# Handing out per-node factors by a matmul: fp32 operands replaced by three exact bf16 parts

## The reference, cut to what matters

```
h        = einsum('ni,hio->hno', layernorm(x), W)
z        = leaky_relu(attn_src[:, src] + attn_dst[:, dst])
weight   = exp(z - max(z))
out[dst] = sum over edges of weight / (sum of weight at dst + 1e-10) * h[src]
```

## Time and profile before

| what | value |
|---|---|
| median of 3 runs | 6532.46 us (6529.53 to 6537.09) |
| the profiled execution | 6535.86 us |
| its span, first to last instruction | 6534.1 us |
| mean granted TensorE clock | 0.889 |

### The profile page before, as it was taken

One profiled execution on the slowest core, in us unless ns is written; L12 is line 12 of the kernel. 1 busy time (PEld: TensorE's weight loads), 2 busy tenths in 40 slices (PEclk: granted clock), 3 DMA queues, 4 the chain that ended last, 5 costly groups with the idle time before them and its releaser, 6 DMA issues. The chain is left out here.

```text
span 6534.1 us, 98546 instructions
## 1 busy us (share of the span) xinstructions
PE 5150.2 (79%) x32067; PEld 4637.9 (71%) x32068; DVE 4163.5 (64%) x9813; ACT 1761.5 (27%) x4052; POOL 4122.6 (63%) x4039
## 2 busy tenths in 40 slices
PE   4438999999999999999995666666666666665887
PEld 3328999999999999999994554554455555455887
DVE  6437899899899889989983333343343343334666
ACT  2202444444444444444441000000000000003554
POOL 1357766776777767677654777777777777771111
PEclk9658999999999999999997777777777777787999
DMA  6555555555555565556543444444444444443121
GB/s 190 151 151 150 152 159 151 154 157 150 155 156 155 149 154 159 150 153 159 150 121 92 128 134 127 128 134 126 125 130 123 121 124 119 118 120 107 64 77 49
DMA packets 639144, 877.37 MB, mean 134 GB/s; under 512 B 254782, under 2 KB 447376, under 8 KB 638050
## 3 DMA queue, kind: packets, MB, share of 16 engines
q0 software_dynamic: 183392, 501.66, 27.2%
q1 hardware_dynamic: 424972, 334.16, 19.6%
q10 hardware_dynamic: 30326, 35.87, 1.6%
HBM read 766.70 MB, written 155.49 MB: 141 GB/s over the span
## 5 line engine op out<-in xcount | busy, mean ns | idle before, releaser
L1231 POOL DMA_INDIRECT m_ring<-tab_a,m_src x1764 | 1970.2, 1117 | 849.5 <-issue 489.4
L1849 POOL DMA_INDIRECT eb_rows<-tab_b,eb_src x1764 | 1714.9, 972 | 541.2 <-issue 537.0
L2090 PE MATMUL eb_acc<-eb_rows,eb_S 128*128 128x257 f32 x3528 | 1131.9, 492 | 505.6 <-DMA eb_rows<-tab_b,eb_src 504.4
L2090 PEld LDWEIGHTS eb_acc<-eb_rows,eb_S 128*128 128x128 f32 x3528 | 884.5, 256 | 714.6 <-DMA eb_rows<-tab_b,eb_src 530.8
L1512 PE MATMUL m_acc<-m_V,m_S 128*128 128x264 f32 x3528 | 862.5, 390 | 0.0
L1916 DVE TENSOR_TENSOR eb_sum<-eb_acc,eb_sum 128x257 f32<-128x257 f32 x98 | 41.8, 426 | 1232.2 <-PE eb_acc L2090 1232.2
L1512 PEld LDWEIGHTS m_acc<-m_V,m_S 128*128 128x128 f32 x3528 | 648.4, 192 | 93.0
L1633 ACT ACTIVATE mh_high<-m_ps,bn_b,bn_s 128x256 fp32r<-128x256 f32 x784 | 441.5, 563 | 891.7 <-PE m_ps L533 891.7
L521 DVE TENSOR_TENSOR mh_low<-mh_full,mh_high 128x512 fp32r<-128x512 f32 x784 | 543.3, 693 | 63.8 <-ACT mh_full L1633 49.6
L1622 ACT ACTIVATE mh_full<-m_ps,bn_b,bn_s 128x256 f32<-128x256 f32 x784 | 400.6, 563 | 664.5 <-DVE mh_low L521 342.0
L1307 DVE TENSOR_TENSOR m_V<-m_ring,m_V 128x1280 f32<-128x1280 f32 (+1 forms) x392 | 532.8, 1359 | 13.4
(11 more groups left out here) (367 smaller groups left out, 10539.9 us busy)
## 6 DMA issues: line engine op xcount, KB each, us to landing
m_dstb<-dst_p SPq DMA_DIRECT2D x196, 320.0 KB
m_dstb<-dst_p SPq DMA_DIRECT2D x196, 256.0 KB
buf<-empty SPq DMA_DIRECT2D x49, 771.0 KB
m_ring<-tab_a,m_src POOLq DMA_INDIRECT x1764
eb_rows<-tab_b,eb_src POOLq DMA_INDIRECT x1764, 2.8
xw_stage<-in_L_ffn_w_dram ACTq DMA_DIRECT2D x16, 1024.0 KB, 9.0
over<-b_blank SPq DMA_DIRECT2D x9, 1452.0 KB, 15.3
mOV<-over SPq DMA_DIRECT2D x49, 264.0 KB, 4.8
```

The lines of the kernel that those rows point to most:

```text
L1231: gp.indirect_dma_start(out=ring[:, j, :], out_offset=None, in_=scratch["tab_a"], in_offset=bass.IndirectOffsetOnAxis(ap=src[:, j:j + 1], ...
L1849: gp.indirect_dma_start(out=rows_[q.par][j][:, t, 0:D], out_offset=None, in_=scratch["tab_b"], in_offset=bass.IndirectOffsetOnAxis(ap=src_ ...
L2090: last_i = nc.tensor.matmul(ps_acc[j][:, 0:NR], S[q.par][j][:, t, :], rows_[q.par][j][:, t, :], start=t == 0, stop=t == WT - 1)
```

## The change

The 16 factors are no longer kept as fp32 for the fused stage: in `bounds`, after the second list is made and before the remaining weight pieces are split, five DVE instructions cut `q` into three bf16 numbers whose sum is the fp32 number (`split_q`). The fp32 `q` lives only through the early phases. The mask `ST` becomes bf16 and keeps the order of the list, so that it is read and written without a step, and a piece of it is now a stationary operand whose columns lie five or four bf16 numbers apart. The hand-out of a piece becomes three bf16 matmuls, which are added in PSUM, each with its own weight load of the same mask. Four pairs of small tiles are also put in one tile each, without another effect on the instructions.

```
-            k["q"] = sbuf(first, "q", [P, NT + 1, 2 * H])
+            k["q3"] = sbuf(first, "q3", [P, NT, 3, 2 * H], BF16)
...
+                k["q"] = sbuf(early, "q", [P, NT + 1, 2 * H])
...
+            def split_q():
+
+                v.wait_ge(q_ok, 2)
+                q, part = k["q"][:, 0:NT, :], [k["q3"][:, :, i, :] for i in range(3)]
+                step(nc.vector.tensor_copy(part[0], q))
+                step(nc.vector.tensor_tensor(q_left[:, :, :], q, part[0], SUB))
+                step(nc.vector.tensor_copy(part[1], q_left[:, :, :]))
+                step(nc.vector.tensor_tensor(q_left[:, :, :], q_left[:, :, :], part[1], SUB))
+                step(nc.vector.tensor_copy(part[2], q_left[:, :, :]))
...
             make_list(1, blist)
+            split_q()
             for n in range(4, len(stages)):
                 lower(n)
...
-    ST = [sbuf(ctx, f"m_ST{i}", [P, QUARTERS[i], P]) for i in pair]
+    ST = [sbuf(ctx, f"m_ST{i}", [P, P, QUARTERS[i]], BF16) for i in pair]
...
-                nc.vector.tensor_scalar(
-                    ST[s.side][:, 0:s.size, :], dstb[s.side][:, 0:s.size * P].rearrange("q (p c) -> q c p", c=s.size),
-                    node_col[s.par][:, :], None, ALU.is_equal).then_inc(ST_ok, 1)
+                nc.vector.tensor_scalar(ST[s.side][:, :, :].rearrange("q p c -> q (p c)"), dstb[s.side][:, 0:s.size * P],
+                                        node_col[s.par][:, :], None, ALU.is_equal).then_inc(ST_ok, 1)
...
-                    last_i = nc.tensor.matmul(psE[s.side][:, j * 16:j * 16 + 2 * H], ST[s.side][:, j, :],
-                                              k["q"][:, s.n, :], start=True, stop=True)
+                    for i in (2, 1, 0):
+                        last_i = nc.tensor.matmul(psE[s.side][:, j * 16:j * 16 + 2 * H], ST[s.side][:, :, j],
+                                                  k["q3"][:, s.n, i, :], start=i == 2, stop=i == 0)
```

More of the change, by code:

```diff
@@ L591, in bounds @@
     zm = sbuf(ctx, "b_zm", [P, 2])
+    q_left = sbuf(ctx, "b_q_left", [P, NT, 2 * H])
     corr = k["corr"]
@@ L1120, in attend_mix @@
     lg = [sbuf(ctx, f"mlg{i}", [P, GM, NX]) for i in pair]
-    lm = [sbuf(ctx, f"mlm{i}", [P, GM]) for i in pair]
-    ls = [sbuf(ctx, f"mls{i}", [P, GM]) for i in pair]
     wg = [sbuf(ctx, f"mwg{i}", [P, GM, NX]) for i in pair]
@@ L1126, in attend_mix @@
     mv = [sbuf(ctx, f"mmv{i}", [P, GM, 2]) for i in pair]
-    ve = [sbuf(ctx, f"mve{i}", [P, GM]) for i in pair]
-    rs = [sbuf(ctx, f"mrs{i}", [P, GM]) for i in pair]
+    ve, rs, lm, ls = ([x[:, i, :] for i in pair] for x in (sbuf(ctx, "m" + n, [P, 2, GM]) for n in ("ve", "rs", "lm", "ls")))
     h1 = [Split(sbuf, ctx, f"mh1{i}", [P, KB, T2]) for i in pair]
```

## The result

The median of four runs is 6387.68 us (6378.63 to 6391.94), the ratio to the kernel before 0.9775 with an interval of 0.9760 to 0.9791. The change makes the kernel faster by 2.25%, 145 us; 201 were forecast. The profiled execution took 6378.63 us, its span 6376.8, the granted clock was 0.886. Of its 157 us against the profiled execution of before, 152.7 lie between the first and the last output bias, so in the fused stage.

What follows compares the result with a forecast made beforehand. PE was taken to set the fused stage's period. The profiled 6535.86 us, less 208 for the hand-out matmuls, plus 7 for the split, gave 6335, so 6331 for the median; the 8-in-10 range was 6290 to 6450.

Steps and rivals of the forecast that it cites:

- What bounds the kernel: Fused stage: PE sets the group's period of 60.55 us, DVE stands 10% below, POOL 14%.
- The pair: Hand-out on PE: a strided bf16 load and matmul takes 27 ns, the contiguous price, against 0.103 us for fp32 before.
- The rule weighed against it: Skill on PE weight loads: packed or strided columns load fast, supporting 27 ns; its general figure is 107 ns for 128.
- The exit's 0.09 us: First two fp32r pairs behind a hand-out take 0.32 instead of 0.23 us; this delay was left as it is.
- The mask: On DVE, beside PE: 1.412 and 0.682 us fall to 553 and 486 ns, 4.2 us a group, priced at nothing.
- part 1: Hand-out matmuls on PE's path: 0.556 us less a quarter on average, 375 times, 208 us in all.
- The split: Five DVE instructions in `bounds`, on the path: 7 us more, nothing hides them; between 3 and 10.
- The first: Rival: strided mask loads on PE stay at 0.103 us a pair, slower than before, 6715 us; chance 0.13.
- The second: Rival: the step doubles PE's load cost, pairs of 50 ns, 6447 us; chance 0.12.
- The third: Rival: DVE takes over, mask at one number a cycle, or POOL loses its slack to the masks: 6387 us; chance 0.12.
- What would show it: Output bias every 56 us, pairs 25 to 29 ns, POOL's staging wait about a third; wrong if pairs exceed 40 ns.

Runs made afterwards that it cites:

- experiments 9 and 10: A small GpSimd addition behind each quarter's gathers, on the changed kernel with one matmul a piece (6449.77 us) and with 128 consecutive edges a piece (6457.94 us).
- experiment 2: Changed kernel with the bf16 mask written piece by piece again, so each piece's load is contiguous and the mask slow: 6417.49 us.
- experiment 3: Changed kernel with mask columns 6, 2, 8 and 16 bf16 numbers apart and the first part of q used three times: 6447.76 us.

## Why the prediction was right or wrong

- **What bounds the kernel: right.** PE set the period before and sets it after; what its hand-outs lost, the group lost: from the start of each of their matmuls to the next start they took 7.38 us a group before and 4.11 after, 3.27 less, and the period is 3.31 shorter. Two readings were a little off, and nothing hangs on them: PE reaches nine tenths from the fifth slice, not the fourth, and the stretch to 3500 us reaches past the stage; up to 3200 us POOL's pauses before the change are 9.9 us a group, not 9.4, and DVE's waits 4.1, not 4.6. That POOL's wait for staging was slack holds too: the additions of experiments 9 and 10 used it up whole.
- **The pair: the mechanism right, the price wrong; this is the term that was mis-sized.** I took the 27 ns of contiguous columns for columns 8 and 10 bytes apart, with the argument that a 16-byte step costs VectorE nothing. VectorE's reading says nothing about TensorE's weight load: measured are 35 and 41 ns. Nor was the reading right: it set the mask (682 ns with a 16-byte step) against another kind of instruction (685), and without the step the mask takes 495. The bounds were right (27 to 103), the choice at their lower end was not. In the sum it is 208 - 152.7 = 55 us of the 57 by which the median lies above the forecast.
- **The rule weighed against it.** By their step, strided bf16 loads take 26 to 63 ns a pair. The Trainium skill ("TensorE: Matmul & The Clock Gate", "Weight-path perf modes") says that columns may be packed or strided; here strided columns are loaded faster than fp32 ones, but not at the packed price from four numbers on. Its general figure for a load (section "LDWEIGHTS"), 107 ns for 128 columns, is not reached at any step. The page agreed with my choice but names no price for a step, and there was no row that did.
- **The exit's 0.09 us: right.** It is still there (0.32 for the two fp32r pairs).
- **The mask: right within 5%.** 580 and 495 ns against 553 and 486. It was right too that it buys nothing by itself and is the cover for part 1: without it (experiment 2) the group takes 58.12.
- **The split: the right size, the wrong exposure.** 6.7 us as worked out, at the place named; but "nothing hides them" was wrong, only 2 to 3 of them reach the end of the phase. I had "3 if ACT's loads catch up" as an end of the range and did not take it.
- **The rivals.** The first is out: no bf16 step reaches 68 ns. The second names the mechanism, a step that makes the load dearer, at 50 ns; the truth lies between it and the forecast. The third has the measured time, 6387, by accident: the mask is not at one number a cycle and PE never runs dry. A time that fits a rival is not its proof; PE's idle time and the length of the mask were the rows to ask.
- **What would show it.** The pairs just passed the bound that I had set for being wrong (40 ns) in the quarters of five. POOL's wait for staging shrank to 43%, not to a third, in keeping with the smaller gain.

## What to carry to other kernels

A stationary operand in bf16 may have a step of two numbers for nothing here; from four on each load pays for the step (35 ns at four, 63 at eight and more, against 26), so measure the pair at the very step that the layout gives. If an order serves the engine that writes a tile and hurts the one that reads it, look for the third way: another dealing of the same data (here of the edges) gave both at once. And where the bound sinks by a few per cent, the next engines are close: here TensorE at 57.3 us had GpSimd and VectorE at some 54 behind it, and the last matmuls removed returned less than half of their time, before either of these was reached, since TensorE then waited for VectorE in single places.

## What the hardware showed that was not expected

- An fp32 stationary operand pays for a step about twice: a pair takes 212 ns at a step of five numbers (222 at four) against 103 without one.
- The price of a bf16 load rises with the step between four and eight numbers by some 7 ns for each number and is flat from eight to sixteen. The Trainium skill ("SBUF — State Buffer", "Door 1: The DMA port swizzle") says that SBUF is read in lines of 16 bytes and that a stride is free up to 8 bf16 numbers. The lines fit these rows: 128 columns touch 64, 80, 96, 128 and 128 of them at steps of 4, 5, 6, 8 and 16, and at the 0.49 ns of the last an estimate by them is 31, 39, 47, 63 and 63 ns, against 35, 41, 45, 63 and 63 measured. The free stride does not fit: the price begins at four. No run here tried a step between two and four or one beyond sixteen.
- The mask's speed on VectorE hangs on the step of the int32 operand that it reads: without one 483 to 495 ns for 512 numbers, with 16 bytes 682, with 20 bytes 1412 for 640 against 563 to 580. Whether fp32 or bf16 is written makes 3% at most (563 and 580 ns), and a step in what is written makes as little (579 and 511 ns in experiment 3).
